# A four-stage transformer kernel: softmax-attention stacks loaded inside the projection, Taylor attention rewritten, row statistics merged in the loops

## The chip, the cores and the metric

The kernel runs on one core of a Trainium2 chip. The metric is the device time of one execution in microseconds (us). The median of 3 runs of the kernel before is 1115.69 us (1115.14 to 1118.65).

## The reference

x has 16 batches of 256 tokens of 128 channels, 4096 tokens in all; everything is float32. Four sublayers follow each other, each with its residual and a layer norm without gain:

```
x = layernorm(x + L0_attn(x))   # causal softmax attention, 16 heads of 8, rotary q and k, @ Wo + bo
x = layernorm(x + L0_ffn(x))    # top 2 of 8 experts per token, clipped GLU, weights = softmax of the 2 logits
x = layernorm(x + L1_attn(x))   # causal linear attention, 16 heads, q and k of 16, v of 8
x = layernorm(x + L1_ffn(x))    # 8 experts choose 512 tokens each: layernorm, 128->512 gelu ->128, scatter-add

# L1_attn: y = sum_j f(q).f(k_j) v_j / (sum_j f(q).f(k_j) + eps) over j <= i, f the degree-2 Taylor feature map,
# so that f(q).f(k) = 1 + s + s*s/2 with s = q.k/4
```

1 + s + s²/2 is (1 + (1 + s)²)/2, so the kernel takes the square of (1 + s) of each masked score and adds the plain causal sum of v, for numerator and denominator alike.

## The kernel before, in words

`program` calls the stages one after the other. Each stage is one block, in which every engine runs a list of its own, held together by semaphores; at its end all engines meet. Tokens lie in 32 tiles of 128 (`NTILE`) and 8 chunks of 512 (`NCH`, `CH`); x stays in SBUF as `xn`.

**`project_layer0`** (line 105). A loop over 8 chunks, two in flight. PE multiplies the chunk `xc` by `wqk`, which gives q and k and their rotated partners in PSUM. DVE multiplies these by `rot` (L230) and adds them (L237, `roped`). ACT and POOL then split `roped` into three bf16 parts, hi, mid and lo (L255, L277, L258, L281), into `parts`. SP stores them to DRAM, `scratch_q` and `scratch_k`, one DMA each per chunk (L168), and loads the chunk after next into `xc` (L160). v goes to `v_all` (L206, L260). The wait of DVE for all constants (`s_w` at 112: `wqk`, `rot`, `wv`, `wo`, `bo`, `tri`, `upper`, queued in that order around the first two `xc` and the four constant rows of the stacks) stands ahead of its first item.

**`attend_softmax`** (line 2052). 32 units of 8 heads, two per batch. q and k come back from DRAM as stacks `qst`, `kst`: the parts of 8 dims each under one another, in the order that lets one matmul form the exact product of split numbers. `load(b)` issues twelve DMAs on SP for one batch (L2136): for q and k, for even and odd heads, runs of 3, 2 and 1 parts of 8 partitions. Four batches (`BUFS` 8 units) fit. For each unit, three fills of scores are reduced to row maxima by DVE (L2319, L2322), these are split, transposed (L2252) and copied to `a_mT` (ACT L2374), and SP puts them as three more rows into `qst` (L2144), so that the scores of the second pass (L2181, L2187) arrive with the maximum already subtracted. ACT takes the exponential (L2370), POOL masks (L2411), PE weights v, transposes and projects. This runs `LEAD` = 3 units ahead with its maxima. SP's order at the start is: stacks of batches 0 to 3, the 16 constants of later stages (L2150), then the `a_mT` copies, and in the loop `a_mT` copies and the next batch's stacks in turn. POOL adds `bo` to all of `xn` in one instruction (L2438).

**Norm, `merge_stats`, `invert_spread`** (lines 2015, 1995, 2003). At the end of a stage DVE merges the statistics of all 32 tiles (L1999). Then a block of its own (or, for norm d, the output block) inverts the spread: DVE adds eps, ACT takes the root with its Sqrt table (L2049), DVE takes the reciprocal and one Newton step (L2040 to L2045).

**`expert_layer0`** (line 786). Its front normalises the tiles, DVE all four of chunks 0 to 2 and three of each later chunk (L1000), POOL the fourth there (L1217), after POOL has cleared `m_wtp`, 128x4096 bf16 (L1213). PE transposes them (L879), ACT copies (L1132); then comes the loop of 64 pairs of expert and chunk.

**`attend(softmax=False)`** (line 292), the Taylor attention. 32 units again, four stack buffers of one unit, six DMAs per unit from `scratch_q`, `scratch_k` of layer 1. Per unit PE makes three tiles of scores (L448, L452), ACT squares them (L713), POOL masks them (L751), PE weights v (L470, L474) into the one tile `a_ps_pv`, ACT copies it to `a_outT` (L693), PE turns it with four transposes (L487), DVE adds the causal sums of v (L615), guards and inverts the denominator and multiplies. The sums of v are three products per batch with 144 columns (L497 to L499), copied by ACT (L699). Per batch there are two transposes (L509), a projection (L517), the residual (L637) and the statistics (L643).

`score_tokens` (1417) and `write_output` (1921) end in the same way, with `merge_stats`; `project_layer1`, `choose_tokens`, `expert_layer1` aren't changed in what they do.

## Time and profile before

| what | us |
|---|---|
| median of 3 runs (lowest, highest) | 1115.69 (1115.14, 1118.65) |
| the profiled execution, its span | 1117.81, 1116.1 |
| projection 0, to | 74 |
| softmax attention, to | 321 |
| norm a, expert stage 0, to | 558 |
| norm b, projection 1, to | 628 |
| Taylor attention, to | 806 |
| norm c, scoring, norm y, to | 840 |
| choice of tokens, expert stage 1, to | 1077 |
| output, to | 1116 |

| engine | busy, share of the span |
|---|---|
| PE | 727.9, 65% |
| DVE | 624.4, 56% |
| ACT | 530.7, 48% |
| POOL | 491.0, 44% |

The ends of the stages are read from the timeline. The shares are averages over eight stages; which engine or queue sets the pace is another question in each. A row of the timeline groups equal instructions that follow each other; the bracket tells how long the engine had been idle and what released it. SPq is SyncE's queue: its durations are the time to issue a DMA, not to move the data.

### The profile page before, as it was taken

What the parts mean: (1) busy time and instruction counts of PE and PEld (TensorE: products, weight loads), DVE (VectorE), ACT (ScalarE), POOL (GpSimd) and SP (SyncE); (2) the same over time, 40 slices, a digit from 0 to 9 for tenths busy, and PEclk for the clock granted to TensorE, in tenths of its full rate; (3) what the DMA queues carried; (4) which work ended last, traced back from release to release, by engine and by line L of the source; (5) the groups of instructions that cost most, each with busy time, mean ns of one, the idle gap of its engine ahead of it and who ended that gap; (6) DMA issues with size and microseconds to landing.
All of it is one profiled execution on the core that took longest, in us unless ns stands there. A gap on an engine that the chain in (4) does not pass through costs nothing. (4 is left out here: it accounts for less than half of the span.)

```text
span 1116.1 us, 20000 instructions
## 1 busy us (share of the span) xinstructions
PE 727.9 (65%) x6532; PEld 411.1 (37%) x6532; DVE 624.4 (56%) x1502; ACT 530.7 (48%) x849; POOL 491.0 (44%) x594
## 2 busy tenths in 40 slices
PE   3822578888847899999768499999681112386700
PEld 1411244444423344444233256556370111254500
DVE  2943468677556877777766223233477789321214
ACT  1420456666625666666457477777421006422102
POOL 0871346555542455555336444444208100468831
PEclk8965689999969999999989699999855555599955
DMA  7533322222000000000036899888006200144454
GB/s 156 177 118 90 108 67 69 66 73 71 6 1 1 0 1 1 1 1 1 1 113 213 204 186 181 150 155 155 2 0 193 75 1 1 27 89 91 60 116 124
DMA packets 138476, 87.72 MB, mean 79 GB/s; under 512 B 10722, under 2 KB 134050, under 8 KB 138274
## 3 DMA queue, kind: packets, MB, share of 16 engines
q1 hardware_dynamic: 132770, 82.57, 30.7%
q0 software_dynamic: 5632, 4.20, 2.8%
q8 instruction: 42, 0.69, 0.3%
q14 instruction: 32, 0.26, 0.1%
HBM read 56.99 MB, written 29.36 MB: 77 GB/s over the span
## 5 line engine op out<-in xcount | busy, mean ns | idle before, releaser
L1211 POOL TENSOR_TENSOR m_prod<-m_upc,m_gatec 128x512 f32<-128x512 f32 x64 | 99.6, 1557 | 114.7 <-DVE m_upc L1063 114.7
L2370 ACT ACTIVATE a_prob<-a_ps_pair 128x1024 f32<-128x1024 f32 x96 | 96.5, 1023 | 59.8 <-PE a_ps_pair L2181 56.8
L2411 POOL TENSOR_SCALAR_AFFINE_SELECT a_prob<-a_prob 128x512 f32<-128x512 f32 (+1 forms) x96 | 75.5, 787 | 105.7 <-ACT a_prob L2370 105.1
L2319 DVE TENSOR_REDUCE a_mx<-a_ps_pair 128x4 f32<-128x1024 f32 x64 | 78.0, 1223 | 77.6 <-PE a_ps_pair L2222 77.5
L751 POOL TENSOR_SCALAR_AFFINE_SELECT a_prob<-a_prob 128x512 f32<-128x512 f32 (+1 forms) x96 | 75.5, 787 | 97.3 <-ACT a_prob L713 97.3
L713 ACT ACTIVATE a_prob<-a_ps_b 128x1024 f32<-128x1024 f32 x96 | 98.6, 1029 | 31.2 <-PE a_ps_b L448 29.5
L1798 POOL DMA_INDIRECT m_y<-normed,m_idx x32 | 31.0, 970 | 103.2 <-DVE m_idx L1886 93.7
L1153 ACT ACTIVATE m_gate<-m_ps_g,bgu 128x512 f32<-128x512 f32 x64 | 43.9, 686 | 53.5 <-PE m_ps_g L914 53.4
L937 PE MATMUL m_ps_d<-m_act,wd 128*128 128x512 f32 x128 | 65.6, 594 | 2.3 <-DVE m_act L1073 2.3
L914 PE MATMUL m_ps_g<-m_x1T,wgu 128*128 128x512 f32 x128 | 65.8, 596 | 0.0
L916 PE MATMUL m_ps_u<-m_x1T,wgu 128*128 128x512 f32 x128 | 65.4, 592 | 0.0
L1603 ACT ACTIVATE c_far<-iota,c_pos 128x128 f32<-128x128 f32 x64 | 19.6, 388 | 86.1 <-DVE c_thr L1733 85.9
L2181 PE MATMUL a_ps_pair<-qst,kst 58*128 58x256 bf16 x256 | 26.5, 290 | 49.6 <-DMA qst<-a_mT 44.7
L1815 POOL DMA_INDIRECT sum<-m_o,m_idx x32 | 50.3, 1573 | 16.3 <-issue 8.8
L1874 ACT ACTIVATE m_hT<-m_ps_h,w 128x512 f32<-128x512 f32 x32 | 22.0, 687 | 69.9 <-PE m_ps_h L1836 69.6
L1406 POOL TENSOR_TENSOR p_parts<-p_resid,p_parts 128x512 bf16<-128x512 f32 x32 | 36.3, 1155 | 38.7 <-ACT p_parts L1386 38.7
L448 PE MATMUL a_ps_b<-qst,kst 96*128 96x256 bf16 x256 | 39.6, 277 | 16.0 <-DMA kst<-scratch_k 16.0
L615 DVE TENSOR_TENSOR a_total<-a_ps_a,a_vsum 128x72 f32<-128x72 f32 x64 | 11.9, 228 | 67.9 <-PE a_ps_a L487 67.9
L1158 ACT ACTIVATE m_up<-m_ps_u,m_bup 128x512 f32<-128x512 f32 x64 | 44.0, 687 | 10.2 <-PE m_ps_u L916 10.1
L470 PE MATMUL a_ps_pv<-a_prob,a_v_now 128*32 128x256 f32 x512 | 40.9, 391 | 12.1 <-ACT a_outT L693 10.5
L1614 POOL TENSOR_SCALAR c_yn<-xn,stats_y,norm_y_rstd 128x128 f32<-128x128 f32 x32 | 27.6, 876 | 42.5 <-POOLq L2005 42.5
L1073 DVE TENSOR_TENSOR m_act<-m_ps_w,m_glu 128x512 f32<-128x512 f32 x64 | 44.2, 691 | 2.2
(281 smaller groups left out, 1818.2 us busy)
## 6 DMA issues: line engine op xcount, KB each, us to landing
scratch_q<-p_parts SPq DMA_DIRECT2D x16, 384.0 KB, 2.6
scratch_k<-p_parts SPq DMA_DIRECT2D x16, 384.0 KB, 2.6
qst<-scratch_q SPq DMA_DIRECT2D x32, 192.0 KB, 3.3
kst<-scratch_k SPq DMA_DIRECT2D x32, 192.0 KB, 4.0
w<-in_w SPq DMA_DIRECT2D x8, 578.0 KB
qst<-scratch_q SPq DMA_DIRECT2D x64, 64.0 KB, 3.5
kst<-scratch_k SPq DMA_DIRECT2D x64, 64.0 KB, 4.0
qst<-scratch_q SPq DMA_DIRECT2D x32, 128.0 KB, 3.4
```

The source lines that it names most:

```text
L713: nc.scalar.activation(prob[:, (3 * s + j) % 6, :], ps_b[(3 * s + j) % 2][:, :], ACT.Exp if softmax else ACT.Square, scale=scale, bias=0.0 ...
L751: nc.gpsimd.affine_select(out=blk, in_=blk, compare_op=ALU.is_ge, fill=0.0, base=0, pattern=[[0, n], [1, P]], channel_multiplier=-1).then_ ...
L914: nc.tensor.matmul(ps_g[n % 2][:, :], wgu[:, e, 0, :], xc, start=True, stop=True).then_inc(s_g, 1)
L916: nc.tensor.matmul(ps_u[n % 2][:, :], wgu[:, e, 1, :], xc, start=True, stop=True).then_inc(s_u, 1)
L937: nc.tensor.matmul(ps_d[:, :], wd[:, e, :], act[:, n % 2, :], start=False, stop=e == E - 1, skip_group_check=True).then_inc(s_dn, 1)
L1073: nc.vector.tensor_tensor(act[:, u, :], ps_w[u][:, :], glu[:, u, :], ALU.mult).then_inc(s_act, 1)
L1158: nc.scalar.activation(up[:, n % 2, :], ps_u[n % 2][:, :], ACT.Identity, bias=bup[:, n % E:n % E + 1]).then_inc(s_uc, 1)
L1211: nc.gpsimd.tensor_tensor(prod[:, n % 2, :], upc[:, n % 2, :], gatec[:, n % 2, :], ALU.mult).then_inc(s_pr, 1)
L1815: nc.gpsimd.indirect_dma_start(out=sum_d[a % 2], out_offset=bass.IndirectOffsetOnAxis(ap=idx[:, e, a:a + 1], axis=0), in_=o[:, e % 2, a, : ...
L2319: nc.vector.reduce_max(mx[:, w % 2, :, 2 * f:2 * f + 2, 1:2], pair[p][:, :].rearrange("p (m h k) -> p m h k", m=2, h=2), AX_X).then_inc(s_ ...
L2370: nc.scalar.activation(prob[:, r % 6, :], pair[(0, 2, 1)[j]][:, :], ACT.Exp, scale=scale, bias=0.0).then_inc(s_e, 1)
L2411: nc.gpsimd.affine_select(out=blk, in_=blk, compare_op=ALU.is_ge, fill=0.0, base=0, pattern=[[0, n], [1, P]], channel_multiplier=-1).then_ ...
```

## The change

**Projection.** SP's order is written out. The constants are asked for in the order of use, with `rot` third; DVE waits only for `rot` before its first item and makes `tri4` after it. The load of x is four quarters, issued at chunks 3 to 6. The parts are stored in four slots, mid, hi, hi, lo, with two DMAs each for q and k per chunk. After the stores of chunk 2 SP waits for them and issues the stack loads of batches 0 and 1, after those of chunk 3 the ones of batches 2 and 3 (`load_stacks`, 32 DMAs in all).

**Softmax attention.** `load_stacks` has eight DMAs per batch, of 32 and of 16 partitions; the first four batches are there already. The 16 later constants are issued two per even unit from u = 2 on. `bo` is added by POOL per batch. DVE merges the statistics of a batch in the loop and inverts the spread at the end of the block.

**Norm.** The inverse root is a shifted integer seed and three Newton steps, twelve dependent DVE instructions, in the block of the stage before; no engine but DVE takes part. ACT's instruction stream has two table loads instead of eight.

**Expert stage 0.** Of each chunk's four tiles DVE normalises two, ACT one, POOL one. `m_wtp` is 128x1024 and cleared after POOL's fourth tile. Merges at e == 6.

**Taylor attention.** `attend_taylor` takes the place of `attend`: unrolled, two output tiles `a_ps_x`, into which the causal sums of v are accumulated by products with `seen` ahead of the weighted v; two transposes per unit instead of four; no `a_vsum`, no additions. The copies out of PSUM (`a_outT`, `a_attT`) are DVE's, the v tiles POOL's, and ACT has the squares only. The stack loads are as before.

The core of the diff (the function that is new is cut to its order of work):

```diff
+MID_HI_LO = (1, 0, 2)
+NSTORE = 4
+RUNS0 = {"q": ((0, 0, 4), (4, 0, 2)), "k": ((0, 0, 2), (2, 0, 4))}
...
+def load_stacks(sp, b, stacks, scratch, done):
+    s, t0 = 2 * b % BUFS, T * (b % 2)
+    for name, st, sc in (("q", stacks[0], scratch[0]), ("k", stacks[1], scratch[1])):
+        src = sc[b // 2, :, :, :].rearrange("s (d h) t -> (s d) h t", h=H)
+        for m in range(2):
+            for s0, part, n in RUNS0[name]:
+                r0 = 64 * m + HD * s0
+                sp.dma_start(st[r0:r0 + HD * n, s:s + 2, :, :].rearrange("p s i t -> p (s i) t"),
+                             src[HD * part:HD * (part + n), m:H:2, t0:t0 + T]).then_inc(done, 16)
...
 project_layer0, SP
-                with sp.Fori(0, NCH // 2 - 1) as k:
-                    for u in range(2):
-                        sp.wait_ge(s_vp, 2 * k + u + 1)
-                        load(2 * k + u + 2, u)
-                        store(2 * k + u, u)
+                for c in range(NCH):
+                    if c + 2 < NCH:
+                        load(c + 2)
+                    store(c)
...
+                    if c in (2, 3):
+                        for i in range(2):
+                            sp.wait_ge(s_store[2 * (c % 2) + i], 32)
+                        for b in (2 * c - 4, 2 * c - 3):
+                            load_stacks(sp, b, stacks, scratch, s_first)
 project_layer0, DVE
-                ve.wait_ge(s_w, 112)
-                for i in range(4):
-                    nc.vector.tensor_copy(tri4[:, i, :], tri_f[:, :]).then_inc(s_tri, 1)
+                ve.wait_ge(s_rt, 16)
...
 attend_softmax, SP
-                for b in range(BUFS // 2):
-                    load(b)
-                for name, dst in consts["later"].items():
-                    sp.dma_start(dst[tuple(slice(None) for _ in dst.shape)], io[name]).then_inc(s_later, 16)
                 for u in range(1 - LEAD, NU):
                     if u + 2 < NU:
                         max_rows(u + 2)
                     if u % 2 == 1 and 0 <= u and u + BUFS < NU:
-                        load((u - 1 + BUFS) // 2)
+                        sp.wait_ge(s_b, 3 * u + 3)
+                        load_stacks(sp, (u - 1 + BUFS) // 2, stacks, scratch, s_st[(u - 1) // 2 % (BUFS // 2)])
+                    if u >= 2 and u % 2 == 0:
+                        for name, dst in later[u - 2:u]:
+                            sp.dma_start(dst[tuple(slice(None) for _ in dst.shape)], io[name]).then_inc(s_later, 16)
 Norm
+        step(nc.vector.tensor_scalar(self.ve[:, :], self.stats[:, :, 1], EPS, None, ALU.add))
+        step(nc.vector.tensor_scalar(self.t[:, :].bitcast(I32), self.ve[:, :].bitcast(I32), 1, None, ALU.logical_shift_right))
+        step(nc.vector.tensor_scalar(self.rstd[:, :].bitcast(I32), self.t[:, :].bitcast(I32), -1.0, float(RSQRT_SEED), ALU.mult, ALU.add))
+        for _ in range(3):
+            step(nc.vector.tensor_tensor(self.t[:, :], self.rstd[:, :], self.rstd[:, :], ALU.mult))
+            step(nc.vector.scalar_tensor_tensor(self.t[:, :], self.t[:, :], -0.5, self.ve[:, :], ALU.mult, ALU.mult))
+            step(nc.vector.scalar_tensor_tensor(self.rstd[:, :], self.t[:, :], 1.5, self.rstd[:, :], ALU.add, ALU.mult))
 expert_layer0, POOL
-                nc.gpsimd.memset(wtp[:, :, :], 0.0).then_inc(s_wz, 1)
                 for c in range(NCH):
-                    if by_pool[c]:
...
+                    if c == 3:
+                        nc.gpsimd.memset(wtp[:, :, :], 0.0).then_inc(s_wz, 1)
 attend_taylor, PE
+                for u in range(NU + 2):
+                    b = (u - 3) // 2 if u % 2 == 1 and u >= 3 else None
+                    if u < NU:
+                        scores(u, 0)
+                        scores(u, 1)
+                    if 0 <= u - 1 < NU:
+                        weighted(u - 1)
+                    if u < NU:
+                        scores(u, 2)
+                    if b is not None:
+                        transpose_att(b)
+                    if u + 1 < NU:
+                        prefix(u + 1)
+                    if 0 <= u - 1 < NU:
+                        turn_out(u - 1)
+                    if b is not None:
+                        project(b)
```

SP in the softmax attention before: the stack copies of batch 3, the last of the four that stand ahead of everything, the constants, and the first `a_mT` copies. A row is line, operation, destination<-source, shape (partitions first).

```order
L2136 DMA kst<-scratch_k 24x8x256
L2136 DMA kst<-scratch_k 16x8x256
L2136 DMA kst<-scratch_k 8x8x256
L2150 DMA wr<-in_wr 128x32
L2150 DMA sel<-in_sel 128x1024
...
L2150 DMA row<-in_row 128x1
L2150 DMA gb<-in_gb 128x2
L2144 DMA qst<-a_mT 3x8x128 x8
L2136 DMA qst<-scratch_q 24x8x256
```

In the change the copies of these four batches stand in the projection, between its stores and its `xc` loads: here from the end of chunk 2 to the start of chunk 3's stores.

```order
L172 DMA scratch_k<-parts 128x2x512 x2
L177 DMA kst<-in_krows 10x32x256 x2
L106 DMA qst<-scratch_q 32x8x256
L106 DMA qst<-scratch_q 16x8x256
...
L106 DMA kst<-scratch_k 16x8x256
L106 DMA kst<-scratch_k 32x8x256
...
L165 DMA xc<-in_xT 128x512
L172 DMA scratch_q<-parts 128x2x512 x2
```

And in the attention, the `a_mT` copies stand first, with the first batch's worth of stacks and two constants behind them.

```order
L1658 DMA qst<-a_mT 3x8x128 x8
L106 DMA qst<-scratch_q 32x8x256
L106 DMA qst<-scratch_q 16x8x256
...
L106 DMA kst<-scratch_k 16x8x256
L106 DMA kst<-scratch_k 32x8x256
...
L1658 DMA qst<-a_mT 3x8x128 x2
L1670 DMA wr<-in_wr 128x32
L1670 DMA sel<-in_sel 128x1024
L1658 DMA qst<-a_mT 3x8x128 x2
```

What had stood between the start of the attention and the first `a_mT` copy now stands in the projection (copies) or behind (constants).

PE in the Taylor attention before, an even unit: tiles of its own scores in `a_ps_b`, weighted v of the unit before and of its own in `a_ps_pv`, the sums of v of its batch in `a_ps_m`, and the turned output of the unit before in `a_ps_a`.

```order
L448 MATMUL a_ps_b<-qst,kst 128x256 x4
L470 MATMUL a_ps_pv<-a_prob,a_v_now 32x256 x4
L497 MATMUL a_ps_m<-a_v_now,upper 128x144
L498 MATMUL a_ps_m<-a_v_now,ones_sq 128x144
L499 MATMUL a_ps_m<-a_v_now,upper 128x144
L448 MATMUL a_ps_b<-qst,kst 128x256 x4
L474 MATMUL a_ps_pv<-a_prob,a_v_now 32x128 x8
L452 MATMUL a_ps_b<-qst,kst 128x128 x8
L470 MATMUL a_ps_pv<-a_prob,a_v_now 32x256 x4
L487 MATMUL a_ps_a<-ident,a_outT 128x128 x4
```

PE in an even unit of the change (`a_ps_pair` scores, `a_ps_x` weighted v of the unit before and sums of v for the next one, `a_ps_y` turned output):

```order
L2059 MATMUL a_ps_pair<-qst,kst 128x256 x8
L2086 MATMUL a_ps_x<-a_prob,a_v_now 32x256 x8
L2092 MATMUL a_ps_x<-a_prob,a_v_now 32x128 x8
L2063 MATMUL a_ps_pair<-qst,kst 128x128 x8
L2073 MATMUL a_ps_x<-a_seen,a_v_row 128x256
L2074 MATMUL a_ps_x<-a_seen,a_v_row 128x128
L2101 MATMUL a_ps_y<-ident,a_outT 128x128 x2
```

The weighted products of a unit now stand together, behind two tiles of the next unit's scores; two products with `a_seen` and two transposes stand where four transposes and, per batch, three products with `upper` and `ones_sq` did.

## Rows read from the trace of the kernel before

**Rows 1.** Timeline, projection of layer 0; columns: start us, duration us, engine, line, operation, [idle before <- releaser]

```profile
20.82 0.63 DVE L223 CAST tri<-tri_f 128x128 bf16<-128x128 f32 x4 [16.52 <-DMA upper<-in_upper]
...
29.15 0.44 SPq L168 DMA_DIRECT2D scratch_q<-parts  x1
...
70.04 0.37 SPq L168 DMA_DIRECT2D scratch_q<-parts  x1
```

**Rows 2.** Timeline, start of the softmax attention

```profile
74.88 4.64 SPq L2136 DMA_DIRECT2D qst<-scratch_q  x6
...
86.63 2.36 DVE L2319 TENSOR_REDUCE a_mx<-a_ps_pair 128x4 f32<-128x1024 f32 x2 [9.49 <-PE a_ps_pair L2222]
...
119.00 3.05 SPq L2144 DMA_DIRECT2D qst<-a_mT  x4
...
122.39 1.94 ACT L2370 ACTIVATE a_prob<-a_ps_pair 128x1024 f32<-128x1024 f32 x2 [25.28 <-PE a_ps_pair L2181]
```

**Rows 3.** Timeline of SP alone, inside the softmax attention's loop

```profile
205.53 3.02 SPq L2144 DMA_DIRECT2D qst<-a_mT  x4
...
217.55 3.02 SPq L2144 DMA_DIRECT2D qst<-a_mT  x4
```

**Rows 4.** Timeline of ACT, end of the softmax attention's loop: units 26 to 29

```profile
281.19 1.94 ACT L2370 ACTIVATE a_prob<-a_ps_pair 128x1024 f32<-128x1024 f32 x2 [2.69 <-PE a_ps_pair L2181]
...
286.99 2.07 ACT L2370 ACTIVATE a_prob<-a_ps_pair 128x1024 f32<-128x1024 f32 x2 [0.30 <-PE a_ps_pair L2181]
...
295.85 2.17 ACT L2370 ACTIVATE a_prob<-a_ps_pair 128x1024 f32<-128x1024 f32 x2
```

**Rows 5.** Busy time of each engine in two stretches (us, busy (instructions) each)

```profile
287.00:297.00 10.00, 9.45 (x188) 5.46 (x184) 8.81 (x14) 7.67 (x12) 6.50 (x17) 1.00 0.03 6
700.00:720.00 20.00, 18.58 (x232) 11.85 (x224) 6.83 (x30) 15.52 (x23) 9.11 (x13) 1.00 0.88 157
```

**Rows 6.** Timeline, ends of three stages: norm a, norm b, norm c

```profile
319.49 2.22 DVE L1999 BATCH_NORM_AGGREGATE stats<-a_bns 128x2 f32<-128x6 f32 x32
...
322.85 0.18 DVE L2038 TENSOR_SCALAR norm_a_ve<-stats 128x32 f32<-128x32 f32 x1 [1.15 <-PEq L83]
...
326.10 3.51 POOL L1213 MEMSET m_wtp<- 128x4096 bf16 x1 [13.72 <-POOLq L2005]
326.15 5.64 DVE L1000 TENSOR_SCALAR xn<-xn,stats,norm_a_rstd 128x128 f32<-128x128 f32 x8 [0.53 <-PEq L2005]
...
555.87 2.22 DVE L1999 BATCH_NORM_AGGREGATE stats<-m_bns 128x2 f32<-128x6 f32 x32
...
563.04 0.48 DVE L1333 MEMSET v_all<- 128x512 f32 x1 [1.03 <-PEq L2005]
...
804.19 2.22 DVE L1999 BATCH_NORM_AGGREGATE stats<-a_bns 128x2 f32<-128x6 f32 x32
...
809.87 1.11 DVE L1478 TENSOR_SCALAR g_x<-xn,stats,norm_c_rstd 128x128 f32<-128x128 f32 x4 [0.53 <-PEq L2005]
```

**Rows 7.** Timeline of ACT and of DVE, around norm y

```profile
836.23 0.20 ACT L1501 ACTIVATE gate_act<-g_ps_s 128x32 f32 x1 [2.05 <-PE g_ps_s L1458]
...
840.46 0.29 DVE L1659 TENSOR_SCALAR c_score<-gate_act 128x256 f32<-128x256 f32 x1 [0.53 <-PEq L2005]
```

**Rows 8.** Timeline of DVE, norm d

```profile
1099.96 0.18 DVE L2038 TENSOR_SCALAR norm_d_ve<-stats 128x32 f32<-128x32 f32 x1
...
1101.72 0.19 DVE L1981 SCALAR_TENSOR_TENSOR w_shift<-stats,norm_d_rstd 128x32 f32<-128x32 f32 x1
```

**Rows 9.** Timeline of ACT, first and last unit's first square, Taylor attention

```profile
636.51 1.02 ACT L713 ACTIVATE a_prob<-a_ps_b 128x1024 f32<-128x1024 f32 x1 [4.93 <-PE a_ps_b L448]
...
793.01 1.02 ACT L713 ACTIVATE a_prob<-a_ps_b 128x1024 f32<-128x1024 f32 x1 [0.88 <-PE a_ps_b L448]
```

**Rows 10.** One line's instructions: the stack copies of the softmax attention

```profile
L2136 SPq DMA_DIRECT2D kst<-scratch_k x96: 595/676/1467, 79.6 to 277.3; - x96
```

**Rows 11.** Waits, Taylor attention from 655 to 790: us in total, times, longest

```profile
PE a_ps_pv L470 <- ACT a_outT L693: 9.5, 25, 0.6
```

913 lines of the change are left out of this document (355 added, 558 removed).

## The prediction

> **What bounds the kernel now.** I read the timeline first, cut by stage, because the whole-run shares average over stages with different limits; then, in the two long attention stages, the distance between equal instructions of successive units. (A difference under 0.3%, some 3.3 us, is about what a measurement of this kernel can tell from no change.)
>
> The projection of layer 0 is bound by its own chunk loop after a late start. VectorE (DVE) idles 16.5 us until `upper`, the last of seven constants, lands, and only then rotates the first chunk. The first store follows 8.3 us later, and seven chunks on to the last one take (70.04 - 29.15)/7 = 5.84 us each [rows 1].
>
> The start of the softmax attention is bound by SyncE's queue (SP). From 74.88 it issues 48 stack copies and 16 constants, 44.1 us in all, and only behind these, at 119.00, the first `a_mT` copies, for which the first exponential waits until 122.39. The maxima it needs are taken from 86.63 on: the data are there, the queue is not [rows 2].
>
> The loop is bound by the same queue for most of its length: four `a_mT` copies (3.02 us) and twelve stack copies follow each other without a gap, 217.55 - 205.53 = 12.02 us per pair of units, so a stack copy takes (12.02 - 3.02)/12 = 0.75 us [rows 3]. From the first exponential to that of unit 26 at 281.19 it is 158.8/13 = 12.2 us a pair. Once SP has no more stacks to load, the pair from unit 27 (286.99) to unit 29 (the second of two in the row that starts at 295.85, so at about 297.0) takes 10.0 us [rows 2, 4]. There PE is busy 94% and DVE 88% [rows 5]: a new limit lies only 2 us under the old one.
>
> Each stage ends with a merge of all row statistics, an end of a block, the inverse root with a hop to ScalarE (ACT), and a second end of a block [rows 6, 7, 8]. The Taylor attention runs at (793.01 - 636.51)/31 = 5.05 us a unit [rows 9], with PE busy 93%, ACT 78%, and the DMA engines 88% [rows 5].
>
> **Projection and first exponential (-26.6).** DVE now waits only for `rot`, which is queued third. PE has its data long before, so the first item starts with the first products, about 9 us sooner (21.5 becomes 12 to 13). Against that, SP issues more inside the loop: four stores of two parts per chunk instead of two of three, 16 extra at 0.37 to 0.44 (the stores of the old loop [rows 1]), which fit into the 5.84 us of a chunk; and 32 stack copies, 32 x 0.75 = 24 us, in two bursts of 16. Behind each burst stand the next `xc` load and the next stores. The `xc` buffers are two deep, so of 12 us of burst the loop absorbs one chunk, about 6; with the wait for the stores to land (under the 4.8 us from the last `scratch_q` store to the next stage [rows 1, 2]; I take 3) each burst costs 8 to 9 us. So the end moves by -9 + 17.3 = 8.3, and the attention starts at 83.2 where it was 74.88. Then its stacks are there. The prologue is some 2.3 us to the first product, eight reductions of maxima at 1.18 (2.36 for two [rows 2]) with their small gaps, 9.8, and 0.5 to the exponential: 95.8 instead of 122.4. Bounds: the bursts hidden wholly, a start at 66, but then the queue of the second burst shows: not under 80 for the exponential (-42); or neither burst hidden at all, 24 + 5 us on top of 62, a start at 91 (-19).
>
> **Softmax attention loop (-22.9).** Eight copies per batch instead of twelve, and two constants at 0.5 in each of eight pairs (16 of them and 48 copies at 0.75 make the 44.1 us above). SP's work per pair is 8 x 0.75 + 3.02 + 1.0 = 10.0 us. DVE's is 8.8 [rows 5] plus two merges at 2.22/32 = 0.07 [rows 6] and their waits; the `bo` addition, 8.8 us of POOL at the start, is now sixteen pieces of about 0.55 on POOL, which is busy 65% [rows 5]. So neither SP nor DVE is far under the 10.0 of the free pair. I take 10.4 per pair, and 11.4 for the first, for two limits of 10.0 that wait on each other: 95.8 + 11.4 + 12 x 10.4 = 232.0 for unit 26, against 281.2; less the 26.6 above, -22.6 to -22.9. Ends: 10.0 (-28) and 11.2 (-13). What a copy of 32 partitions costs to issue no row shows. The nearest are the copies of 24, 16 and 8 partitions, 0.595 to 1.467 us with a median of 0.676 [rows 10], with no order by size that I can see; I take the mean, 0.75. SP becomes the limit again from (10.4 - 3.02 - 1.0)/8 = 0.80 us a copy.
>
> The Trainium skill, page "DMA: Bandwidth & Descriptors", section "Why a DMA increments its semaphore by 16 and not by 1", gives in a table for generations before the newest 512 sequencer cycles per copy instruction, with no term for shape. By that rule a copy costs the same for 32 partitions as for 8, and the term stands; this trace agrees for the stores alone (0.37), since stack copies differ among themselves and take twice that.
>
> **Ends of stages (-11.1).** A merge now runs in the loop for each batch, so 0.15 is left of 2.22; the inverse root is twelve DVE steps at 0.22 (the old chain's 1.76 us for eight [rows 8]), 2.7 us; and one end of a block, 1.15 (the idle time ahead of the row at 322.85 [rows 6]), instead of two. Norm a: 319.49 to 326.15 is 6.66, now about 4.0, -2.6 [rows 6]. Norm b: 555.87 to 563.04 is 7.17, now 4.2, -3.0. Norm c: 804.19 to 809.87 is 5.68, now 4.2, -1.5. Norm y: the last tanh to the first score of the next block, 836.23 to 840.46, is 4.23; the inversion now lies on an idle DVE while ACT and PE finish, 0.9 is left, -3.3 [rows 7]. Norm d: merges of the last quarter alone, but more steps, -0.7 [rows 8]. The merges cost their loops nothing while DVE has idle time, which the Taylor attention has in plenty (6.8 of 20 us busy [rows 5]). Ends: -7 and -14.
>
> **Front of the expert stage (-4).** POOL's memset of 3.51 us runs beside DVE's normalising, and eight DVE tiles of 128x128 take 5.64 us, where four in the scoring take 1.11, so eight 2.2: 3.4 too much [rows 6]. The memset becomes a quarter and moves behind POOL's first four tiles. Of the 3.4 I take 2.8, since PE's transposes follow the tiles at their own pace; three engines instead of two on the tiles, and a table load gone, perhaps 1.2 more. Ends: 1.5 and 5.6.
>
> The Trainium skill, page "SBUF — State Buffer", section "SBUF: two separate sides", says that VectorE and GpSimd share a port pair which one instruction holds exclusively to its end. The trace agrees: DVE's excess of 3.4 us is near the memset's 3.51. By the page 3.5 would come back there, by the sum above 2.8.
>
> **Taylor attention (-10.8).** PE loses two of four transposes per unit and the three sums of v per pair, and gains two prefix products of 256 and 128 columns: about even. What goes is a wait: PE's weighted products waited for ACT's copy out of the one output tile, 9.5 us in 135 [rows 11], 0.35 a unit; ACT now does only squares, the copies go to DVE, and the output tile is doubled. 5.05 becomes 4.7, times 31. Ends: 5.05, where PE is full anyway, and 0.88 x 5.05 = 4.45, where the DMA engines are [rows 5].
>
> **Sum.** -26.6 - 22.9 - 11.1 - 4 - 10.8 = -75.4, from 1117.81 of the profiled execution (span 1116.1, 1.7 lie around it) to 1042.4. The median of the runs shown, 1115.69, is 2.1 lower, so 1040 to 1042: I say 1041.
>
> **Rivals.**
> - Taylor attention stays at 5.05, because PE at 93% has no wait that really ends: 1052. For it speaks PE's load, against it the named wait. Chance 0.18.
> - The bursts hold the projection up by 10 us more, because each delay of an `xc` load also delays the stores behind it: 1051. Chance 0.12.
> - The price of issuing goes with the partitions moved: the eight copies cost what the twelve did, 8.9 us a pair, 1.11 each. The projection grows by 11 more, the pairs stay at 12.0, plus 1.0 in eight of them: unit 26 at 107 + 156 + 8 = 271. That leaves -10 - 25.9: about 1082. Against it speaks that the row of copies shows no such growth [rows 10]. Chance 0.07.
> - All at the good ends, DVE's 8.8 setting the pair near 10.0 and the bursts half hidden: 1028 or less. Chance 0.10.
> - Slower than before: every copy of the new shape issues at 1.47, the longest of the row [rows 10]. The bursts take 47 us, the attention starts at 106, its first exponential is at 119, a pair takes 8 x 1.47 + 3.02 + 1.0 = 15.8 (14.8 without constants), unit 26 comes at 319, 38 late; less the other 26, 1130. It decides from about 1.35 us a copy. Chance 0.02; another 0.01 for a result inside 0.3%, between these two.
>
> The forecast itself has 0.50. The range: 1022 to 1066 leaves out the two dear-copy cases and the far end of the good one, less than 0.2. Chances: faster 0.97, same 0.01, slower 0.02.
>
> **What would show it.** First store near 20; the stack copies in two bursts of about 12 us; the attention's first exponential at 90 to 100; pairs at 10.0 to 10.8 with gaps in SP's row; units of the Taylor attention at 4.7 with no wait for a copy out; 2.7 us of DVE chain per norm and no ScalarE in it. Copies over 0.8 us, or an unchanged Taylor pace, prove the sum wrong in these places; a DVE over 95% busy in the softmax loop would say that the merges are not hidden.

## The result, and the profile after

The changed kernel takes 1048.64 us (median of 4 runs, 1045.85 to 1052.09), the kernel before 1117.17 (4 runs, 1115.14 to 1120.32): a ratio of 0.9386, 95% interval 0.9347 to 0.9424. The forecast was 1041, within 1022 to 1066. The gain is 68.5 us instead of 74.7. The sum came out near, and its terms did not: two of them are off by 9 to 10 us, in opposite directions, and three of the five lie outside their own bounds.

The spans of the two profiled executions, 1116.1 and 1047.6, cut at the same instructions:

| stretch | before | after | change | forecast |
|---|---|---|---|---|
| start to the first exponential | 122.4 | 106.2 | -16.2 | -26.6 |
| to the exponential of unit 26 | 158.8 | 133.7 | -25.1 | -22.9 |
| to the merge that begins norm a | 38.3 | 37.2 | -1.1 | 0 |
| norm a | 6.7 | 4.1 | -2.6 | -2.6 |
| expert stage 0 | 229.7 | 228.7 | -1.0 | -4 |
| norm b | 7.2 | 4.7 | -2.4 | -3.0 |
| projection 1, to the first square | 73.5 | 74.4 | +0.9 | 0 |
| Taylor attention, first to last unit's first square | 156.5 | 136.8 | -19.7 | -10.8 |
| its tail, norm c, scoring, norm y | 47.4 | 42.8 | -4.6 | -4.8 |
| choice, expert stage 1 (code unchanged), to the output's first statistics | 243.7 | 247.0 | +3.3 | 0 |
| output with norm d | 31.9 | 31.9 | 0.0 | -0.7 |

The rows that answer to [rows 1, 2]: SP's timeline in the projection, then ACT's at the first exponential (106.19 where it was 122.39), both of the changed kernel.

```profile
19.97 0.90 SPq L172 DMA_DIRECT2D scratch_q<-parts  x2
...
37.79 3.27 SPq L106 DMA_DIRECT2D qst<-scratch_q  x4
...
49.10 0.60 SPq L165 DMA_DIRECT2D xc<-in_xT  x1
...
53.28 4.26 SPq L106 DMA_DIRECT2D qst<-scratch_q  x4
...
65.33 0.60 SPq L165 DMA_DIRECT2D xc<-in_xT  x1
...
89.43 0.90 SPq L172 DMA_DIRECT2D scratch_k<-parts  x2
```

```profile
106.19 1.02 ACT L1893 ACTIVATE a_prob<-a_ps_pair 128x1024 f32<-128x1024 f32 x1 [1.27 <-PE a_ps_pair L1697]
```

The first store is at 19.97, 9 us sooner, as forecast. The bursts last from 37.8 to 49.1 and from 53.3 to 65.3. PE starts the attention at 94.0, where the sum had its start at 83.2 and its bad bound at 91.

PE's timeline shows what each burst did: a load of x issued behind it at 49.10 and at 65.33, and PE waited for it.

```profile
55.48 6.54 PE L220 MATMUL ps_b<-xc,wqk 128*128 128x512 f32 x8 [9.32 <-DMA xc<-in_xT]
...
71.46 5.38 PE L220 MATMUL ps_b<-xc,wqk 128*128 128x512 f32 x8 [8.55 <-DMA xc<-in_xT]
```

Four stretches of the changed kernel (us, busy (instructions) of PE, PEld, DVE, ACT, POOL, then the granted clock, the DMA share and GB/s):

```profile
40.00:45.00 5.00, 5.00 (x8) 2.07 (x7) 1.98 (x3) 0.24 (x1) 1.32 (x2) 0.58 1.10 154
50.00:60.00 10.00, 4.52 (x6) 1.94 (x7) 0.70 (x2) 0.66 (x2) 1.74 (x2) 0.55 1.02 254
240.00:250.00 10.00, 9.62 (x191) 5.73 (x188) 8.80 (x16) 7.61 (x11) 7.25 (x18) 1.00 0.02 5
700.00:720.00 20.00, 19.42 (x271) 14.69 (x272) 7.60 (x30) 13.41 (x15) 12.87 (x22) 1.00 1.21 163
```

In the first two the DMA share is over 1 and the granted clock is 0.58 and 0.55 of full speed, near the lower of TensorE's two levels: PE has waited, and its next products run slower. In the third, the softmax loop, PE is busy 96%, where it was 94% in the free pair before [rows 5]. In the fourth, the Taylor attention, it is 97%, where it was 93%.

The softmax loop's pairs, on ACT (unit 26, unit 28): 10.14 us, with nothing that waits for SP.

```profile
239.93 1.02 ACT L1893 ACTIVATE a_prob<-a_ps_pair 128x1024 f32<-128x1024 f32 x1 [0.57 <-PE a_ps_pair L1697]
...
250.07 1.94 ACT L1893 ACTIVATE a_prob<-a_ps_pair 128x1024 f32<-128x1024 f32 x2 [0.57 <-PE a_ps_pair L1697]
```

A cost that the forecast doesn't name stands at the start, on DVE and POOL. The four casts to `tri4`, which took 0.63 us before the first item [rows 1], now stand behind it, where POOL works:

```profile
16.62 4.52 DVE L259 CAST tri<-tri_f 128x128 bf16<-128x128 f32 x4
...
16.52 2.31 POOL L296 TENSOR_TENSOR resid<-roped,parts 128x512 f32<-128x512 f32 x2 [16.01 <-ACT parts L274]
```

They take 4.52 us and end when POOL's four instructions end, at 21.1. In the other executions of kernels with the change they take from 0.6 to 4.6 us, and in those whose projection is this one the attention starts up to 2.5 us sooner or 3.4 later than here. So a difference of 2 or 3 us in this stage, between single executions, shows nothing.

Norm a on DVE, answering to [rows 6]: the last merge, the first of the twelve steps, one end of a block, the first tile, 4.08 us in all. The tiles take 0.3 us each again.

```profile
277.13 0.25 DVE L1560 BATCH_NORM_AGGREGATE stats<-a_bns 128x2 f32<-128x6 f32 x2
277.41 0.18 DVE L1571 TENSOR_SCALAR norm_a_ve<-stats 128x32 f32<-128x32 f32 x1
...
281.21 0.62 DVE L524 TENSOR_SCALAR xn<-xn,stats,norm_a_rstd 128x128 f32<-128x128 f32 x2 [1.15 <-PEq L76]
```

The Taylor attention on ACT, answering to [rows 9]: (725.88 - 589.04)/31 = 4.41 us a unit.

```profile
589.04 1.94 ACT L2207 ACTIVATE a_prob<-a_ps_pair 128x1024 f32<-128x1024 f32 x2 [11.83 <-PE a_ps_pair L2059]
...
725.88 1.94 ACT L2207 ACTIVATE a_prob<-a_ps_pair 128x1024 f32<-128x1024 f32 x2 [0.61 <-PE a_ps_pair L2059]
```

So there were three questions: what the stack copies cost in the projection, why the Taylor attention gained nearly twice the forecast, and whether the smaller terms had their reasons.

### The profile page after: what moved, and what is told of

It reads as the page before. It is cut to its first block and busy times, and to the rows that moved or that the text cites. A ratio compares the mean times of both kernels' runs of the same rounds, so it can differ in the third digit from the quotient of the medians.

```text
span 1047.6 us, 19006 instructions
## 1 busy us (share of the span) xinstructions
PE 725.9 (69%) x6490; PEld 423.3 (40%) x6500; DVE 622.7 (59%) x1476; ACT 492.3 (47%) x766; POOL 506.0 (48%) x661
## 5 line engine op out<-in xcount | busy, mean ns | idle before, releaser
L2207 ACT ACTIVATE a_prob<-a_ps_pair 128x1024 f32<-128x1024 f32 x96 | 94.8, 1022 | 57.6 <-PE a_ps_pair L2059 37.9
L1893 ACT ACTIVATE a_prob<-a_ps_pair 128x1024 f32<-128x1024 f32 x96 | 96.4, 1023 | 13.8 <-PE a_ps_pair L1697 11.0
L692 ACT ACTIVATE m_gate<-m_ps_g,bgu 128x512 f32<-128x512 f32 x64 | 43.9, 686 | 55.0 <-PE m_ps_g L438 54.9
L220 PE MATMUL ps_b<-xc,wqk 128*128 128x512 f32 x64 | 39.0, 763 | 31.5 <-DMA xc<-in_xT 21.7
L2149 DVE COPY a_outT<-a_ps_x 128x256 f32<-128x256 f32 x32 | 13.6, 425 | 57.1 <-PE a_ps_x L2092 57.1
L585 DVE TENSOR_SCALAR m_gatec<-m_gate 128x512 f32<-128x512 f32 x64 | 30.5, 477 | 25.9 <-ACT m_gate L692 25.7
L1439 DVE TENSOR_SCALAR m_yT<-m_ps_x,gb 128x512 f32<-128x512 f32 x8 | 6.5, 810 | 64.4 <-PE m_ps_x L1376 64.4
```

What stands on the lines that cost most here:

```text
L692: nc.scalar.activation(gate[:, n % 2, :], ps_g[n % 2][:, :], ACT.Identity, bias=bgu[:, n % E, 0:1]).then_inc(s_gb, 1)
L1893: nc.scalar.activation(prob[:, r % 6, :], pair[(0, 2, 1)[j]][:, :], ACT.Exp, scale=scale, bias=0.0).then_inc(s_e, 1)
L2207: nc.scalar.activation(prob[:, r % 6, :], pair[r % 2][:, :], ACT.Square, scale=scale, bias=1.0).then_inc(s_e, 1)
```

## The experiments

All are the changed kernel with one edit, but for those said to have more. Up to the versions at the end each time is that of one execution, and each experiment is read in its own stage of that execution.

**The stack copies in the projection.** First taken out of it:

```diff
 project_layer0, SP
-                    if c in (2, 3):
-                        for i in range(2):
-                            sp.wait_ge(s_store[2 * (c % 2) + i], 32)
-                        for b in (2 * c - 4, 2 * c - 3):
-                            load_stacks(sp, b, stacks, scratch, s_first)
 attend_softmax, SP
+                for b in range(BUFS // 2):
+                    load_stacks(sp, b, stacks, scratch, s_st[b])
```

> The changed kernel, with the 32 stack copies of the first four batches issued by SP at the start of the softmax attention and none in the projection. Read: the start of the attention (93.9 in the changed kernel's trace) and the first exponential (106.2). Theory A, the two bursts hold the projection up by more than they save: without them chunks follow each other every 5.8 us from the first store near 20, the attention starts at 66 to 68, the copies take 32 x 0.60 to 0.75 = 19 to 24 us, the first exponential comes at 90 to 96, and the whole is 10 to 16 us shorter. Theory B, the copies were hidden in the projection, whose length has another cause: the attention still starts later than 85, and the first exponential moves to 115 or later, 10 us or more longer.

Measured: 1041.07 us, span 1039.3. The attention starts at 74.1 and the first exponential is at 99.25. SP at the start of the attention, and ACT:

```profile
74.13 2.64 SPq L106 DMA_DIRECT2D qst<-scratch_q  x4
...
95.83 3.09 SPq L1652 DMA_DIRECT2D qst<-a_mT  x4
...
99.25 1.94 ACT L1889 ACTIVATE a_prob<-a_ps_pair 128x1024 f32<-128x1024 f32 x2 [7.44 <-PE a_ps_pair L1693]
```

Theory A holds in its direction: with the 21.7 us of copies in plain view at the start, the first exponential is still 6.9 us sooner than with the copies "hidden" in the projection. They made the projection 20 us longer (last store at 70.05 instead of 89.8), and little there absorbed them. But the chunks don't follow each other every 5.8 us: from the first store to the last it is 49.8 us, where the kernel before took 42.0. SP and PE of this run show why:

```profile
29.84 1.40 SPq L177 DMA_DIRECT2D qst<-in_qrows  x2
31.28 0.47 SPq L165 DMA_DIRECT2D xc<-in_xT  x1
```

```profile
38.01 6.59 PE L214 MATMUL ps_b<-xc,wqk 128*128 128x512 f32 x8 [4.10 <-DMA xc<-in_xT]
```

The constant rows of the stacks, which stood ahead of everything before, now go out inside the loop, and the load of x issued behind them at 31.28 reaches PE at 38.0. PE waits 4.1 us, and the chunk's products of 512 columns (four in the code, x8 in the rows) then take 6.59 us instead of the 3.60 of most other chunks. In the kernel before these rows stood ahead of the constants that DVE waited for until 20.8; a part of that delay may only have moved.

Then four buffers for x (`xc` four deep, `load(c + 3)` ahead of `store(c)`). The expectation calls this two chunks earlier; in SP's order, where `load(c + 2)` stood there, it is one:

> The changed kernel, with four buffers for the chunks of x in the projection instead of two, each loaded two chunks earlier, so that no load of x stands behind a burst of stack copies when it is needed. Theory A1, the bursts cost time through the loads of x behind them (PE waits of 9.3 and 8.5 us at 55.5 and 71.5 in the changed kernel's trace): these waits go, the attention starts at 80 to 86 instead of 93.9, the whole is 8 to 13 us shorter. Theory A2, they cost it through the stores behind them (the buffers of the parts are two deep and a store waits for the burst): PE's waits on x are replaced by waits for the parts' buffers, and the attention starts at 90 or later.

Measured: 1045.53; the attention starts at 92.0, 2.4 sooner, which is inside the spread of the unchanged projection (DVE's first instruction there at 91.9 to 97.8). Neither theory as stated: the waits are there still, one chunk later.

```profile
56.30 6.50 PE L223 MATMUL ps_b<-xc,wqk 128*128 128x512 f32 x8 [8.97 <-DMA xc<-in_xT]
...
73.93 6.21 PE L223 MATMUL ps_b<-xc,wqk 128*128 128x512 f32 x8 [10.25 <-DMA xc<-in_xT]
```

With two chunks in reserve at each burst instead of one, a load of x still stands behind it, and PE has used up the reserve before that load lands. The edit doesn't do what theory A1 was about, to have no needed load behind a burst, so it doesn't decide between the two theories.

Then, with the four buffers, eight copies behind each of chunks 2 to 5:

> As the four buffers for x, and the 32 stack copies spread: eight behind the stores of each of chunks 2 to 5 instead of sixteen behind chunks 2 and 3. If only SP's issue time counts: eight copies at 0.61 make 4.9 us beside four stores of 1.8, one load of 0.5, in a chunk of 5.84: some 1.5 us more in each of four chunks, start of the attention at 72 to 76, first exponential at 84 to 88, the whole 18 to 22 us shorter than the changed kernel. If the DMA engines' time counts (busy over 90% from 35 to 75 us in the changed kernel's trace, 32 copies for some 34 us): start at 78 to 84, the whole 10 to 16 shorter.

Measured: 1045.41; last store 80.9, start of the attention at 87.8 (by DVE's first instruction, 94.4 in the changed kernel), first exponential 99.6. This is nearest to the second theory, and later still: SP's issue time at 0.61 a copy would have given 72 to 76. SP has no gap from 36.4 to 81.7, but its own issues have grown: eight copies take 6.6 to 6.8 us instead of 4.9. The DMA share is 0.9 to 1.1 there. That full DMA engines stretch the issues is the likely reading; no run separates the two.

**The number of copies.** The runs of four parts cut into three and one, so that a batch has twelve copies again:

```diff
-RUNS0 = {"q": ((0, 0, 4), (4, 0, 2)), "k": ((0, 0, 2), (2, 0, 4))}
+RUNS0 = {"q": ((0, 0, 3), (3, 3, 1), (4, 0, 2)), "k": ((0, 0, 2), (2, 0, 3), (5, 3, 1))}
-NLOAD0 = 8
+NLOAD0 = 12
```

> The changed kernel with the same stacks loaded by twelve copies per batch instead of eight (each run of four parts cut into three and one), in the projection too. Theory: SP's issue per copy sets the pace again. At 0.61 to 0.75 a copy, a pair of units takes 12 x 0.61 to 0.75 + 3.0 + 1.0 = 11.3 to 13.0 us with constants, 10.3 to 12.0 without, against 10.13: 8 to 25 us longer over the loop, and the two bursts in the projection 5 us each longer. Rival: a copy's price goes with its partitions, so twelve cost what eight did: the pair stays at 10.1 to 10.3.

Measured: 1090.04, 41 us over the changed kernel: the loop from the first exponential to unit 26 takes 163.7 us instead of 133.7, more than the 8 to 25 expected, a pair 12.6, the attention starts 10 later. From 120 to 235 PE waits 17.0 us for `a_mT` copies, in the changed kernel 0.4. SP has no gap:

```profile
217.55 1.47 SPq L1658 DMA_DIRECT2D qst<-a_mT  x2
219.06 4.30 SPq L106 DMA_DIRECT2D qst<-scratch_q  x6
223.40 4.30 SPq L106 DMA_DIRECT2D kst<-scratch_k  x6
227.74 1.52 SPq L1658 DMA_DIRECT2D qst<-a_mT  x2
229.30 0.42 SPq L1670 DMA_DIRECT2D row<-in_row  x1
229.77 0.42 SPq L1670 DMA_DIRECT2D gb<-in_gb  x1
230.24 1.47 SPq L1658 DMA_DIRECT2D qst<-a_mT  x2
```

230.24 - 217.55 = 12.7 us a pair. This is the whole gain of the loop and more, from one table: the pace was SP's, and the copies set it. The prices of the copies of q (lowest, median, highest, in ns), of the changed kernel (8 per batch, 32 and 16 partitions), then of this run (24, 16 and 8):

```profile
L106 SPq DMA_DIRECT2D qst<-scratch_q x64: 585/602/2313, 37.8 to 231.2; - x64
```

```profile
L106 SPq DMA_DIRECT2D qst<-scratch_q x96: 577/658/1505, 38.0 to 271.3; - x96
```

The median hides that the price goes by the shape. Three copies of k of this run, one by one, of 16, 24 and 8 partitions:

```profile
223.40 0.60 SPq L106 DMA_DIRECT2D kst<-scratch_k  x1
224.04 0.79 SPq L106 DMA_DIRECT2D kst<-scratch_k  x1
224.88 0.68 SPq L106 DMA_DIRECT2D kst<-scratch_k  x1
```

The kernel before has the same three prices, medians of 0.60, 0.79 and 0.68, and in the changed kernel 32 and 16 partitions both take 0.60. It isn't the order of issue: q of this run has its copies of 24 first, then 8, and the same prices. So the change took away a third of the copies and the two dearer shapes with them, and this run brought back both: that the number alone sets the pace, it doesn't show. Twelve copies of 0.60 with `a_mT` copies and constants would still be the longest work of a pair, as an estimate 12 x 0.64 + 3.0 + 1.0 = 11.7 us.

The Trainium skill, page "DMA: Bandwidth & Descriptors", section "Why a DMA increments its semaphore by 16 and not by 1", has in its table one figure per copy instruction for generations before the newest, with no term for shape. The traces agree for 32 against 16 partitions, and not for 24 (0.79), for 8 (0.68) or for the stores (0.37 to 0.50).

**The Taylor attention.** PE's products cut into groups again, as the kernel before had them:

```diff
-                        scores(u, 0)
-                        scores(u, 1)
-                    if 0 <= u - 1 < NU:
-                        weighted(u - 1)
-                    if u < NU:
-                        scores(u, 2)
+                    for j in range(3):
+                        if u < NU:
+                            scores(u, j)
+                        if 0 <= u - 1 < NU:
+                            weighted(u - 1, j)
```

> The changed kernel; in the Taylor attention PE's sixteen weighted products of a unit, which stand together, are cut in three groups (4, 4 and 8 products) with a tile of scores ahead of each, as in the kernel before. Read: the distance of the first squares of successive units, 4.42 us in the changed kernel, 5.05 before. Theory G (grouping): products in groups of four start and end alone; before, 96 of the wide ones took 8.1 us of PE in six units where the changed kernel's took 6.4, and 48 wide scores 7.2 against 6.2, together 0.45 us a unit. So 4.75 to 4.9 a unit, the whole 10 to 15 us longer. Theory W (the wait for the copy out, as the prediction had it): grouping does nothing, 4.42 to 4.5.

Measured: 1070.65; 5.22 us a unit, 0.81 more, 25 us in the stage, above the range of either theory. The stretch from 650 to 670 and a row of its waits from 620 to 700:

```profile
650.00:670.00 20.00, 18.18 (x225) 11.49 (x218) 6.13 (x26) 12.04 (x12) 11.17 (x18) 1.00 0.82 151
```

```profile
PE a_ps_x L2073 <- DVE a_outT L2150: 7.3, 16, 0.6
```

PE's time per unit is 18.18/20 x 5.22 = 4.75 us, where the changed kernel's is 19.42/20 x 4.41 = 4.29 and that of the kernel before 18.58/20 x 5.05 = 4.69 [rows 5]. The same sixteen weighted products and sixteen scores keep PE 0.46 us longer when they stand in small groups. The rest is a wait, 7.3 us in 80: with the last group just ahead of the sums for the next tile, the copy out is no longer covered, although there are two tiles.

Then one output tile instead of two:

```diff
-        ps_x = [ps(f"ps_x{i}", [P, 512]) for i in range(2)]
+        ps_x = [ps("ps_x0", [P, 512])] * 2
...
-                    after(pe, s_ev, u - 1)
+                    after(pe, s_ev, u)
...
-                    if u + 1 < NU:
-                        prefix(u + 1)
+                    if 1 <= u < NU:
+                        prefix(u)
```

> The changed kernel; in the Taylor attention one output tile in PSUM instead of two, so that the sums of v of the next unit wait for DVE's copy of this one. Theory W: the doubled tile was worth the 0.35 us a unit that PE waited before; it comes back, 4.75 to 4.8 a unit, the whole 11 us longer. Theory G: the copy (0.42 us and its latency) is covered by the third tile of scores, 4.42 to 4.55 a unit, the whole 0 to 4 us longer.

Measured: 1060.48; 4.78 us a unit, 0.37 more. The price is theory W's, and the wait is not. PE's sums don't wait for the copy out, which the third tile of scores covers, as theory G had it. With one tile the sums of a unit also come one turn of PE's list later, and POOL, which copies the rows of v for a later batch between its masks, waits for them. Then the masks are late, and the weighted products wait for these:

```profile
POOL a_v_row L2224 <- PE a_ps_x L2074: 11.7, 8, 1.5
PE a_ps_x L2086 <- POOL a_prob L2219: 7.1, 17, 0.7
```

The changed kernel has no wait of the first kind in the same stretch (620 to 700) and 2.0 us in 10 of the second. PE's own time is nearly unchanged (18.10/20 x 4.78 = 4.33).

Then the copy by ACT:

```diff
-                    nc.vector.tensor_copy(outT[:, u % 2, :], ps_x[u % 2][:, 0:T]).then_inc(s_ev, 1)
+                    nc.scalar.activation(outT[:, u % 2, :], ps_x[u % 2][:, 0:T], ACT.Copy).then_inc(s_ev, 1)
```

> The changed kernel; in the Taylor attention the copy of the output tile is made by ACT, between its squares, instead of DVE. Theory W: ACT's copy stands in the queue of the squares, and both PE's turn and the next scores wait for it: 4.6 to 4.8 a unit, the whole 6 to 11 us longer. Theory G: ACT has 3 x 1.02 of squares and 0.4 of copy in 4.42 us, and the tile is double: 4.42 to 4.5, the whole 0 to 3 us longer.

Measured: 1044.63; 4.41 us a unit, the same as with DVE. Who copies doesn't matter here.

**The merges.** Those of the first expert stage taken from the loop to its end:

> The changed kernel; in the first expert stage the row statistics are merged after the last chunk (32 merges, 2.22 us) instead of four per chunk in the loop. In the changed kernel the stage's lead over the one before, 2.5 us after its front, shrinks by about 0.25 us at each chunk and ends at 1.0. Theory M (the merges in the loop lie on the path, through DVE): the lead stays at 2.5, the stage's loop is 1.5 us shorter, its end 1.8 longer, the whole within 0.5 us of the changed kernel. Rival: the drift has another cause (the weights' 32-row transposes, POOL): it stays, and the whole is 1.8 us longer.

Measured: 1052.15. The rival holds. The 64 first ACT instructions of the stage's pairs (L692), counted from the front's first tile, are at the same distances with and without the merges (second at 22.9 and 22.9, last at 219.3 and 219.3), and the end of the stage with norm b is 1.7 longer. The merges cost the loop nothing, and the 0.25 us that each chunk has lost has another cause. The instructions at a chunk's end differ there in the transposes of `m_wtp` alone, now 32 columns wide; that was not tried by itself.

**Constants and the memset.** The 16 constants ahead of the attention's loop again, and a memset of 128x4096 ahead of POOL's tiles in the front of the expert stage:

```diff
+                for name, dst in later:
+                    sp.dma_start(dst[tuple(slice(None) for _ in dst.shape)], io[name]).then_inc(s_later, 16)
                 for u in range(1 - LEAD, NU):
...
-                    if u >= 2 and u % 2 == 0:
-                        for name, dst in later[u - 2:u]:
-                            sp.dma_start(dst[tuple(slice(None) for _ in dst.shape)], io[name]).then_inc(s_later, 16)
 expert_layer0, POOL
+                nc.gpsimd.memset(wide[:, :], 0.0)
```

> The changed kernel with two edits in stages apart, each read in its own stage. (1) The 16 constants are issued at the start of the softmax attention again, ahead of the first a_mT copies. SP is idle there for some 7 us after the start (from 94 to 101.3 in the changed kernel), 16 constants take 16 x 0.48 = 7.7: the first exponential comes 0 to 2 us later after the start than the 11.8 of the changed kernel, and the pairs of units stay at 10.13, since SP no longer sets them; if SP did set them, they fall by up to 1.0 in the first eight. (2) POOL clears an unused tile of 128x4096 bf16 (as the kernel before cleared m_wtp) ahead of its tiles in the front of the expert stage. Theory L (the memset blocks DVE): DVE's first tiles take 3 us more, and the first gate comes 3 to 4 us later after the front's start than 7.8. Rival: POOL's own tile, which now comes 3.5 us later, delays the first chunk by the same; then DVE's tiles keep their 0.3 us each and only PE's transposes wait for POOL.

Measured: 1055.64; some 7 us more than the changed kernel, 3.4 of them a later start of the attention, in code that this edit doesn't touch. The first exponential comes 11.83 us after the start of the block's work (11.78 in the changed kernel), and the pairs stay at 10.14. With SP free at the start, the place of the constants is worth nothing. The memset, in the timeline of POOL and DVE:

```profile
284.34 3.51 POOL L760 MEMSET m_wide<- 128x4096 bf16 x1 [11.13 <-POOLq L76]
284.38 3.61 DVE L525 TENSOR_SCALAR xn<-xn,stats,norm_a_rstd 128x128 f32<-128x128 f32 x2 [1.14 <-PEq L76]
```

Two DVE tiles take 3.61 us, where the same two take 0.62 without it (281.21 above), and the first gate comes 11.0 us after the front's start instead of 7.7. DVE stands still for as long as POOL's memset lasts, as the page "SBUF — State Buffer" of the Trainium skill says in "SBUF: two separate sides". POOL's own first tile also comes 3.5 us later here, so of the 3.3 us at the gate DVE's share isn't separated.

**A version from these readings.** Four buffers for x; only two batches of stacks in the projection, behind chunks 5 and 6; the third at the start of the attention, where SP is idle; the fourth behind the first maximum rows:

```diff
+                    if c in (5, 6):
+                        b = c - 5
+                        for i in range(2):
+                            sp.wait_ge(s_store[i], 32)
+                        load_stacks(sp, b, stacks, scratch, s_first)
 attend_softmax, SP
+                load_stacks(sp, 2, stacks, scratch, s_st[2])
                 for u in range(1 - LEAD, NU):
                     if u + 2 < NU:
                         max_rows(u + 2)
+                    if u == -1:
+                        load_stacks(sp, 3, stacks, scratch, s_st[3])
```

> A version meant to beat the changed kernel: four buffers for x; of the first four batches' stacks only two are loaded in the projection, eight copies each behind the stores of chunks 5 and 6, the third at the start of the attention, the fourth behind the first two sets of maximum rows. If the bursts' harm is as the first experiments showed (the attention started at 74.6 without them, 87.8 with 32 copies spread), the attention starts at 74 to 80, the first exponential follows 11.8 to 12.5 us later, at 86 to 92, and the whole is 14 to 20 us shorter than the changed kernel, 1029 to 1035. If copies of any number late in the projection cost what they did early, the first exponential comes at 97 or later and the gain is no more than the 7 us of loading all stacks at the start.

Measured, in five executions: 1030.49 us (1028.43 to 1034.14), 0.9232 of the kernel before (0.9205 to 0.9258). SP, and the first exponential:

```profile
54.10 2.95 SPq L106 DMA_DIRECT2D qst<-scratch_q  x4
...
62.77 3.05 SPq L106 DMA_DIRECT2D qst<-scratch_q  x4
...
69.75 1.05 SPq L172 DMA_DIRECT2D scratch_k<-parts  x2
77.78 2.50 SPq L106 DMA_DIRECT2D qst<-scratch_q  x4
```

```profile
90.06 1.02 ACT L1897 ACTIVATE a_prob<-a_ps_pair 128x1024 f32<-128x1024 f32 x1 [1.27 <-PE a_ps_pair L1701]
```

The projection is as long as with no stack copy in it (50.1 us from the first store to the last, 49.8 there), and the first exponential is at 90.1 instead of 106.2. But the sixteen copies aren't free. This version has four buffers for x, that run had two, and PE waits for no load of x here. POOL has the last parts ready at 63.2:

```profile
60.97 2.26 POOL L301 TENSOR_TENSOR parts<-resid,parts 128x512 bf16<-128x512 f32 x2
```

SP issues the last store of them at 70.3, because the eight copies behind chunk 6, and the stores before them, stand ahead on the queue: some 7 us. With two buffers and no copies the last parts are ready at 69.6 and the last store follows at 70.05. So the version gains some 7 us by the loop that no longer waits, and gives them back at its end. No run has the last stores ahead of the copies.

The same with the constant rows' loads behind chunks 3 and 4 instead of 1 and 2:

> The same with the four constant rows' loads behind chunks 3 and 4 instead of 1 and 2. In the run without stack copies in the projection the load of x behind these rows took 6.6 us to land and PE waited 4.1 for it. With four buffers for x that wait should be gone in either place: within 2 us of the other version. If the rows' data hold back the stores, it is 2 to 5 us faster or slower.

Measured: 1040.38 (1036.78 to 1044.77), ratio 0.9317 (0.9290 to 0.9345), 10 us slower, worse than any theory here had it. The last store is 8 later. The rows now fall in with the quarters of `in_x`, SP's own issues grow to between 0.7 and 2.3 us each from 47 to 60, and a load of `xn` lands 10 us after its issue. ACT waits for stores to land, 3.4 us at 54.4 and 4.4 at 63.3, before it can write the next parts.

And the changed kernel itself beside them:

> The changed kernel itself, on the same chip as the two versions, so that they can be set against it: 0.935 to 0.942 of the kernel before, 1045 to 1053.

Measured: 1047.15 (1046.67 to 1049.46), ratio 0.9381 (0.9362 to 0.9399). So the first version, with its deeper buffers and its later stacks together, is worth 16.7 us on top of the change.

## Why the prediction was right, and where it was not

- **The whole.** Forecast 1041, measured 1048.6, in the range. That the whole is right is in part luck: the two large misses, +10.4 and -8.9, nearly cancel, and three terms lie outside their own bounds (first exponential -16.2 for -42 to -19, front of the expert stage -1.0 for -5.6 to -1.5, Taylor attention -19.7 with a floor of -18.6). The smaller misses, +3.3 in code that the change doesn't touch among them, make most of the 7 us that are left.
- **Projection and first exponential.** The start of DVE 9 us sooner, and 12.6 us from the start of the attention to the exponential (12.2 measured), are right. What failed is the step from the old loop to the new one. "Of 12 us of burst the loop absorbs one chunk, about 6" is wrong, and so is the wait for the stores to land, which the sum put in its place. SP waits there for the stores of chunks 0 and 1, which the batches read, and not for those just issued, as the text on the change has it; they are long done, and SP doesn't stop. The two wrong halves nearly cancel: 17.3 in the sum, 20.0 measured against the run without copies: 21.3 at the two chunks behind the bursts, of which the next wins 3.4 back, and some 2 beside them. The load of x waits behind the burst in SP's order and lands some 6 us after its issue, and PE comes back at the lower clock. The larger part of the miss is a cost that the sum didn't have and the first experiment showed: 7.8 us more for the seven chunks even without stack copies. 6.0 of it is at the chunk behind the constant rows, which now stand inside the loop, 2.1 at the last chunk, and 0.9 lies in the first three, where the casts meet POOL; the others win 1.2 back. The rival at 0.12, "the bursts hold the projection up by 10 us more", has its number and not its mechanism: of the 10 the bursts made 2.7 at most.
- **Softmax loop.** 10.14 a pair for 10.4, with PE busy 96%, and not two limits that wait on each other. The term was 2.2 us too small (its working gives 22.6, the sum took 22.9). That the copies set the pace before is shown by the run with twelve: 12.7. Constants played no part. The rivals of dear copies are refuted: 0.60 us for 32 and 16 partitions. The mean of 0.75 was too high for them, because the row of all copies hid its three prices: "no order by size" was right, an order by shape is there.
- **Ends of stages.** -2.6, -2.4, -1.6, -2.8 for norms a, b, c, y against -2.6, -3.0, -1.5, -3.3. Norm d took 3.86 instead of 4.01, and the output stage as a whole nothing. Merges in loops are free, as said; the run with the merges last shows it for the expert stage.
- **Front of the expert stage.** The mechanism is shown by the memset put back: 3.3 us. In the profiled execution the first gate comes 3.9 us sooner after the front's start, and the gain shrinks to 1.0 by the end; 1.5 of that is the 0.25 a chunk above. The rest is TensorE's clock. In the second profile of the changed kernel the second gate is at 20.6 after the front's start instead of 22.9, and the stage ends 3.3 sooner than before, against the forecast's 4. PE's products just ahead of that gate, of the first profile and of the second, and the busy times (columns as above) of both stretches:

```profile
295.56 1.91 PE L438 MATMUL m_ps_g<-m_x1T,wgu 128*128 128x512 f32 x2
...
295.50:299.00 3.50, 3.50 (x6) 1.33 (x6) 1.89 (x7) 0.63 (x1) 1.16 (x1) 0.50 0.00 0
```

```profile
293.89 1.02 PE L438 MATMUL m_ps_g<-m_x1T,wgu 128*128 128x512 f32 x2
...
294.00:297.50 3.50, 3.50 (x30) 1.81 (x28) 2.08 (x8) 1.54 (x4) 1.27 (x1) 1.00 0.00 0
```

At a granted clock of 0.50 the same row of products takes 1.91 us instead of 1.02. It goes so in all twelve executions of kernels with the change and without the memset put back: where the clock is 1.00 there, in seven, the second gate is at 20.6 to 21.1, where it is 0.50, in five, at 22.9 to 23.4. So 2.3 us of this stage change with the clock from execution to execution, and at the full clock the stage ends 2.8 to 3.3 us sooner than before, of the forecast's 4. What makes the clock fall in some and not in others stays open.
- **Taylor attention.** Of the 0.63 us a unit, PE's own time is 0.40 (4.69 to 4.29) and PE's idle time 0.23 (0.36 to 0.13). The named wait, 0.35 in the sum, is gone, and shorter waits for the masks have come. What ended it isn't the engine that copies (4.41 with ACT too), and that it is the doubled tile isn't shown: the run with one tile costs 0.37, but through POOL, and the run with two tiles and small groups has the wait back. What the runs show is the order: the third tile of scores stands between the weighted products and the sums and covers the copy. What failed is "about even" for PE's own time. It counted instructions by kind and left out how they stand: in large groups the same products take 0.4 us a unit less. The floor of 4.45 "where the DMA engines are" was none: the stage runs at 4.41 with a DMA share of 1.21, so that share is no measure of a limit here.
- **Open.** The choice of tokens and expert stage 1, whose code is the same, take 247.0 us instead of 243.7, and 244.6 to 247.0 in the twelve other runs of kernels with the change. The difference grows mostly from expert to expert. The granted clock in the four stretches of 40 us from the stage's 60th us on is 0.50, 0.55, 0.96, 0.87 instead of 0.50, 0.58, 1.00, 0.91, which can be cause or consequence; no run was made for it.

## What to carry to other kernels

A load that is moved under other work isn't hidden by that: ask what stands behind it on its queue, both loads that an engine will need and stores that end the stage. Here two bursts of sixteen copies ahead of needed loads cost 18 to 20 us; sixteen copies behind the last load of x kept PE from waiting and still held the last stores by some 7. Where one queue feeds a loop, count DMA issues and take the price of each shape from the trace, not one mean. When products are regrouped, take PE's time from its busy share per unit in each arrangement, not from a count of instructions. And when an edit gives the forecast price, look whether the wait is the forecast one.

## What the runs showed of the hardware

- Issuing one copy takes 0.60 us for 32 and for 16 partitions, 0.68 for 8 and 0.79 for 24 (medians of the kernel before and of the changed one). Single ones took up to 2.3.
- After PE's waits of 3.8 to 10.3 us in the projection of the changed kernel and of the first two runs a chunk's products of 512 columns take 5.4 to 6.6 us instead of 3.6, at a granted clock of 0.54 to 0.68: a wait of 9.3 us costs 12.
- The same kernel gets a clock of 0.50 or of 1.00 at one place of the expert stage, and is 2.3 us slower or not by that.
- PE's work of a Taylor unit, sixteen weighted products and sixteen scores with the rest, takes 4.29 us with these in groups of 8 and 16, 4.75 in groups of 4 and 8.
- A GpSimd memset of 3.51 us stops VectorE's tensor-scalar tiles for its whole length: 3.61 us for two. Four casts of 128x128 beside GpSimd's tensor-tensor instructions took 4.52 us instead of 0.63.
